# Attention values held still on 32-column tiles: weighing the values with the turned probabilities moving, and turning the heads in 32x32 blocks on VectorE

## The chip, the core and the metric

The kernel runs on one core of a Trainium2 chip. The metric is the device time of one execution in microseconds (us). The kernel before takes 1671.57 us, the median of three runs (1671.38 to 1672.91). A core has TensorE (matrix products, from SBUF into PSUM), VectorE, ScalarE, GpSimd, and SyncE, which issues most transfers. Each works through its own queue in the order in which the program is written, and they meet at semaphores.

## The reference: what is computed

Two layers over `x` (128 sequences of 64 tokens, 128 wide). Each layer adds a gated cross-attention to a context of the same shape and then a gated expert layer. Cut to what matters:

```python
q = (layernorm(x) @ Wq + bq).reshape(b, s, 16, 8)      # 16 heads of 8
k = (ctx @ Wk + bk).reshape(b, s, 16, 8)
v = (ctx @ Wv + bv).reshape(b, s, 16, 8)
attn = softmax(mask(q k^T / sqrt(8)))                  # 64 x 64 for each head
x = x + tanh(g_xattn[l]) * (attn v @ Wo + bo)
# layer 0: each token goes to one of 8 experts, 128 -> 512 -> 128, with gelu
# layer 1: each token has 16 weights w[n,e]; q, k, v = sum_e w[n,e] * (x @ P[e]);
#          one 64 x 64 attention per sequence; out = sum_e w[n,e] * (o @ P_o[e])
x = x + tanh(g_ffn[l]) * experts_l(layernorm(x))
```

Everything is float32 in and out.

## The kernel before

The tokens are worked in 32 units of 256 tokens (4 sequences). The program has three stages. Layer 0's attention is a software pipeline with a loop over the units (`body0` on each engine, which works at once on stages of the units u-2 to u+3). Then come 71 slots of 128 tokens through layer 0's experts. Layer 1 is again a pipeline over units (`body1`), in which the 16 expert projections of a unit (`tokens_parts`, three matmuls of 384 columns for each expert and half unit t) stand on TensorE between the steps of the attention of unit u+2 and of the token attention of unit u-1. The order of everything is written out by hand in these bodies, one for each engine; nothing is scheduled by a planner. The waits are `wait_ge` on a semaphore and a count; `Steps` makes each VectorE step of a chain wait for the one before it.

Of the attention of a unit, these steps bear on the change:

- `head_values` makes the values. The keys' tokens (64 columns of `xcT`) are stationary, and the rows of `m0` are (head parity, key). ScalarE's `copy_v` puts them into `vb`, whose 18 columns for each pair of heads (`VW` = 9 for each head) are 8 dimensions and a column of ones for each of the two heads, and zero in the other head's rows.
- `transpose_probs` turns the exponentials `prob[j]` of one quad of heads (j = 0 to 3) into the bank `tb`, and ScalarE's `copy_pT` copies it to `pT`, of which there are two buffers. So a copy waits until the weighing of two quads before has ended.
- `weigh_values(j)` multiplies: 8 products for each quad, the turned probabilities stationary (128 x 64), 18 columns of `vb` moving, into 64 rows of the bank `po`. Rows of `po` are then (half, query), and its columns are (head, dimension and sum).
- VectorE's `normalise` takes the reciprocal of the sums (`rden`) and multiplies (`on`). TensorE turns `on` (`transpose_heads` in layer 0, `upper_heads` in layer 1), ScalarE copies the result to `oT` (`copy_oT`), and `output` multiplies by `Wo`. VectorE's `add_residual` and `second_stats` take it from there. The statistics go to GpSimd (`second_norm`) and then to ScalarE (`apply_second_norm`).

In `body0` VectorE's last step is `normalise(u)`. Its next body begins with `first_stats` of the unit three further on, whose statistics GpSimd turns into a scale and applies (`norm`, `apply_norm`, into `xn`); TensorE's `transpose_in` waits for that. In `body1`, VectorE's `take_part` adds the t = 0 half of a projection to `qkv` out of one of two banks; `part` on TensorE waits until the part two before it has been taken. `token_weights(u-1)` on VectorE normalises the token attention, and TensorE's `token_weights(u-1)` then turns it.

## Time and profile before

| | |
|---|---|
| time, median of 3 runs | 1671.57 us (1671.38 to 1672.91) |
| profiled execution: span from the first to the last instruction | 1668.5 us |
| around the span, by the median | 3.1 us |
| layer 0's attention: values made (L1639) | 13.8 to 342.5 us |
| layer 1: values made (L1639) | 534.8 to 1536.4 us |
| TensorE busy (matmul) over the span | 1592.5 us (95%) |
| VectorE, ScalarE, GpSimd busy | 1206.6, 1079.6, 1179.4 us |

The profiled execution comes with no time of its own beyond its span. TensorE's share of busy time is no measure of how close it is to its peak, since matmuls overlap in the records; how far apart the starts of two groups lie says what the first one costs in the queue.

### The profile page before, as it was taken

The numbers are of one execution on the slowest core, as the hardware profiler recorded it, in microseconds if no ns is written. First come the engines' busy times: TensorE is split into PE (matmuls) and PEld (weight loads), VectorE is DVE, ScalarE is ACT, GpSimd is POOL, SyncE is SP. The second block draws the span as 40 slices with busy tenths as digits, with TensorE's granted clock in tenths as the row PEclk, the third lists the DMA queues.
The fourth block names the chain that finished last, engine by engine and source line by source line (L and its number), as shares of the span: only waits on it lengthen the run. The fifth ranks groups of instructions, "written<-read, shape, count | busy, mean of one in ns | idle before, by whom it ended". The sixth has DMA issues, their size and how long they took to land.

```text
span 1668.5 us, 50902 instructions
## 1 busy us (share of the span) xinstructions
PE 1592.5 (95%) x15977; PEld 1386.3 (83%) x15978; DVE 1206.6 (72%) x3915; ACT 1079.6 (65%) x2725; POOL 1179.4 (71%) x1715
## 2 busy tenths in 40 slices
PE   6999999976999899999999999999999999999996
PEld 4777777756998689888988988888988988898885
DVE  3677777753554568788887888788888888787785
ACT  3777777743555556666666666666666666666654
POOL 3556656642455578887888888887888888887785
PEclk9999999987999999999999999999999999999998
DMA  2322222234542100000000000000000000000000
GB/s 74 109 73 74 76 75 76 80 96 129 146 134 77 29 17 11 17 17 21 14 18 17 17 18 16 17 16 21 14 18 17 18 17 17 16 16 11 5 8 10
DMA packets 92101, 68.95 MB, mean 41 GB/s; under 512 B 13936, under 2 KB 87696, under 8 KB 91920
## 3 DMA queue, kind: packets, MB, share of 16 engines
q1 hardware_dynamic: 76512, 49.34, 10.1%
q0 software_dynamic: 5120, 12.62, 2.4%
q10 hardware_dynamic: 10288, 4.74, 1.1%
q8 instruction: 94, 1.54, 0.4%
q14 instruction: 87, 0.71, 0.1%
HBM read 35.74 MB, written 22.52 MB: 35 GB/s over the span
## 4 chain that ended last, share of the span: by engine, by line
PE 81%; DVE 5%; issue 5%; POOL 5%; DMA 2%; SPq 1%; ACT 1%; POOLq 0%; DVEq 0%; ACTq 0%
PE s_bank L1884 14%; PE s_bank L1885 12%; PE s_bank L1886 12%; PE po L1702 6%; PE tb L1685 5%; PE po L1831 4%; PE s_bank L1819 4%; PE s_bank L1665 3%; PE s_bank L2034 2%; PE m L1639 1%; PE s_bank L2021 1%; PE tb L1884 1%; POOL sorted_in L652 1%; POOL qkv L726 1%; PE m L1935 1%
## 5 line engine op out<-in xcount | busy, mean ns | idle before, releaser
L726 POOL TENSOR_TENSOR qkv<-qkv,scaled 128x384 f32<-128x384 f32 x480 | 490.1, 1021 | 128.8 <-ACT scaled L1009 91.2
L1009 ACT ACTIVATE scaled<-s_bank,wg 128x384 f32<-128x384 f32 x449 | 257.2, 582 | 128.8 <-PE s_bank L1886 127.3
L1884 PE MATMUL s_bank<-proj_hi,hn_hi 128*128 128x384 f32 x900 | 331.4, 368 | 1.3 <-DVE qkv L1451 1.0
L1451 DVE SCALAR_TENSOR_TENSOR qkv<-s_bank,wg,qkv 128x384 f32<-128x384 f32 x449 | 274.2, 611 | 49.6 <-PE s_bank L1886 37.9
L1885 PE MATMUL s_bank<-proj_lo,hn_hi 128*128 128x384 f32 x900 | 303.7, 337 | 0.0
L1886 PE MATMUL s_bank<-proj_hi,hn_lo 128*128 128x384 f32 x900 | 302.1, 336 | 0.0
L869 ACT ACTIVATE pT<-tb 128x512 f32<-128x512 f32 x256 | 152.2, 595 | 148.9 <-PE tb L1685 81.3
L1884 PEld LDWEIGHTS s_bank<-proj_hi,hn_hi 128*128 128x128 f32 x900 | 169.4, 188 | 16.3 <-ACT scaled L1009 5.9
L1885 PEld LDWEIGHTS s_bank<-proj_lo,hn_hi 128*128 128x128 f32 x900 | 170.0, 189 | 3.0
L1886 PEld LDWEIGHTS s_bank<-proj_hi,hn_lo 128*128 128x128 f32 x900 | 169.0, 188 | 0.0
L1685 PE MATMUL tb<-ident,prob 128*128 128x128 f32 x1024 | 157.6, 277 | 4.8 <-ACT pT L869 4.8
L1702 PEld LDWEIGHTS po<-vb,pT 128*64 128x64 f32 x4096 | 138.8, 138 | 22.2 <-issue 22.2
L1702 PE MATMUL po<-vb,pT 128*64 128x18 f32 x4096 | 151.7, 213 | 0.4 <-ACT pT L869 0.4
L1462 DVE SCALAR_TENSOR_TENSOR halves<-s_bank,wg,halves 128x128 f32<-128x128 f32 x448 | 127.3, 343 | 24.5 <-DVE halves L1462 19.7
L1685 PEld LDWEIGHTS tb<-ident,prob 128*128 128x128 f32 x1024 | 117.8, 141 | 29.3 <-issue 19.9
L726 POOL TENSOR_TENSOR sums<-sums,scaled 128x512 f32<-128x512 f32 x96 | 123.4, 1286 | 12.3 <-ACT scaled L1013 6.0
L1013 ACT ACTIVATE scaled<-s_bank,wg 128x128 f32<-128x128 f32 x384 | 109.5, 368 | 24.1 <-PE s_bank L1886 23.8
L956 ACT ACTIVATE prob<-s_bank 128x512 f32<-128x512 f32 x128 | 73.4, 599 | 76.4 <-PE s_bank L2034 76.4
L927 ACT ACTIVATE hT<-s_bank,b_cols 128x128 f32<-128x128 f32 x284 | 81.2, 367 | 62.6 <-PE s_bank L1819 62.5
L652 POOL DMA_INDIRECT sorted_in<-xr,posi x64 | 66.1, 1033 | 63.8 <-DVE posi L1247 51.0
L1405 DVE TENSOR_REDUCE mx<-s_bank 128x8 fp32r<-128x512 f32 x128 | 79.5, 682 | 40.6 <-PE s_bank L1665 40.6
L1182 DVE RECIPROCAL rden<-po 128x32 f32<-128x32 f32 x64 | 22.8, 357 | 114.7 <-PE po L1702 114.7
(291 smaller groups left out, 3816.2 us busy)
## 6 DMA issues: line engine op xcount, KB each, us to landing
xs<-sorted_in SPq DMA_DIRECT2D x71, 128.5 KB, 2.1
kx<-kT SPq DMA_DIRECT2D x256, 32.0 KB, 1.9
sorted_out<-yo SPq DMA_DIRECT2D x71, 64.0 KB, 1.6
xin<-in_x SPq DMA_DIRECT2D x32, 128.0 KB
cin<-in_ctx SPq DMA_DIRECT2D x32, 128.0 KB
ctx_cols<-xcT SPq DMA_DIRECT2D x32, 128.0 KB
w<-in_L_ffn_W SPq DMA_DIRECT2D x16, 256.0 KB
xcT<-ctx_cols SPq DMA_DIRECT2D x32, 128.0 KB, 2.9
```

The lines of the kernel that those rows point to most:

```text
L652: g.indirect_dma_start(out=sorted_in[:, :], out_offset=bass.IndirectOffsetOnAxis(ap=posi[par][:, t:t + 1], axis=0), in_=xr[par][:, t, 0:RO ...
L726: g.tensor_tensor(into, into, scaled[m % SCALED][:, 0:cols], ALU.add).then_inc(dense_added, 1)
L869: act.activation(pT[j % 2][:, :, :, :], tb[:, :].rearrange("p (r t n) -> p r t n", r=2, t=2), ACT.Copy).then_inc(q["probT_ready"], 1)
L1009: ins = act.activation(into, bank[:, 0:3 * D], ACT.Copy, scale=wg[v % 4][:, 1, k:k + 1])
L1013: ins = act.activation(part[:, cols] if k else sums[:, e, :], bank[:, cols], ACT.Copy, scale=wg[v % 4][:, 1, 4 * k + e:4 * k + e + 1])
L1451: v.scalar_tensor_tensor(out=acc, in0=bank[:, 0:3 * D], scalar=wg[w % 4][:, 0, k:k + 1], in1=acc, op0=ALU.mult, op1=ALU.add).then_inc(dens ...
L1462: ins = v.scalar_tensor_tensor(out=into, in0=bank[:, cols], scalar=wg[w % 4][:, 0, e:e + 1], in1=into, op0=ALU.mult, op1=ALU.add)
L1685: ins = pe.transpose(tb[:, col:col + P], prob[j][:, t, 2 * r:2 * r + 2, :], ident[:, :])
L1702: ins = pe.matmul(po[64 * half:64 * half + 64, col:col + 2 * VW], pT[j % 2][:, t, r, 64 * half:64 * half + 64], vb[par][:, seq, 2 * j + r, ...
L1884: pe.matmul(bank[:, 0:cols], hi[:, tile], of(proj_hi), start=True, stop=False)
L1885: pe.matmul(bank[:, 0:cols], hi[:, tile], of(proj_lo), start=False, stop=False)
L1886: pe.matmul(bank[:, 0:cols], lo[:, tile], of(proj_hi), start=False, stop=True)\
```

## The change

Both layers get the same new weighing. `vb` becomes the stationary operand (18 columns) and the turned probabilities move (64 columns). The output of quad j goes to rows 32j to 32j+17 of `po`, which is a column tile of 32 of the array, and all four quads are weighed in one group of 32 products, after all four copies of `pT` (of which there are now four buffers). `po` then holds the heads already turned, but in blocks: VectorE turns it in 32x32 blocks into `turned` (512 columns, from PSUM), takes the reciprocal, multiplies, and turns the 256 columns of `on` again, straight into `oT`. TensorE's two transposes of `on` and ScalarE's copy of `oT` are gone. `head_values` and `token_scores` make the same products with stationary tiles of 32 columns in place of 64, twice as many. `po` is set to zero once at the start. The PE, ScalarE and VectorE orders are rewritten where the hand-written bodies name these steps; VectorE's `body0` keeps its order.

```diff
-        pT = [sb(f"pT{b}", [P, 2, 2, P]) for b in range(2)]
+        pT = [sb(f"pT{j}", [P, 2, 2, P]) for j in range(QUADS)]
+        turned = sb("turned", [P, 2, 8, 32])
...
             def copy_pT(q, u, j):
                 if exists(u):
                     act.wait_ge(q["probT_in_psum"], 4 * u + j + 1)
-                    wait(act, q["pv_in_psum"], 4 * u + j - 1)
-                    act.activation(pT[j % 2][:, :, :, :], tb[:, :].rearrange("p (r t n) -> p r t n", r=2, t=2),
+                    wait(act, q["pv_in_psum"], u)
+                    act.activation(pT[j][:, :, :, :], tb[:, :].rearrange("p (r t n) -> p r t n", r=2, t=2),
...
             def normalise(q, u):
...
-                    v.wait_ge(q["pv_in_psum"], 4 * u + 4)
-                    step = Steps(v, q["vec_rden"], u, 1)
-                    o = po[:, 0:2 * HEADS * VW].rearrange("p (a c) -> p a c", c=VW)
-                    step(v.reciprocal(rden[:, :], o[:, :, HD]))
-                    wait(v, q["oT_in_psum"], u)
-                    v.tensor_tensor(on[:, :, :].rearrange("p t (h d) -> p (t h) d", d=HD), o[:, :, 0:HD],
-                                    bcast(rden[:, :], HD, 2), ALU.mult).then_inc(q["heads_ready"], 1)
+                    v.wait_ge(q["pv_in_psum"], u + 1)
+                    step = Steps(v, q["vec_heads"], u, 3)
+                    step(v.transpose(turned[:, :, :, :].rearrange("p r b c -> p (r b c)"), po[:, :]))
+                    rows = turned[:, :, :, 0:2 * VW].rearrange("p r b (h c) -> p (r b) h c", h=2)
+                    step(v.reciprocal(rden[:, :, :], rows[:, :, :, HD]))
+                    step(v.tensor_tensor(on[:, :, :, :].rearrange("p r b (h d) -> p (r b) h d", h=2),
+                                         rows[:, :, :, 0:HD], bcast(rden[:, :, :], HD, 3), ALU.mult))
+                    step.end()
+                    wait(v, q["y_in_psum"], u)
+                    v.transpose(oT[:, :, :].rearrange("p t n -> p (t n)"),
+                                on[:, :, :, :].rearrange("p r b c -> p b r c")).then_inc(q["heads_ready"], 1)
...
                     for h in range(2):
-                        ins = pe.matmul(m0[64 * h:64 * h + 64, LEN * seq:LEN * seq + LEN],
-                                        xcT[par][:, 1, LEN * seq:LEN * seq + LEN], by_head[:, h, :, :],
-                                        start=True, stop=True, skip_group_check=True)
+                        for part in range(2):
+                            row, key = 64 * h + 32 * part, LEN * seq + 32 * part
+                            ins = pe.matmul(m0[row:row + 32, LEN * seq:LEN * seq + LEN],
+                                            xcT[par][:, 1, key:key + 32], by_head[:, h, :, :],
+                                            start=True, stop=True, skip_group_check=True)
...
-            def weigh_values(q, u, par, j):
+            def weigh_values(q, u, par):
...
                         for r in range(2):
-                            col = 2 * VW * (8 * t + 2 * j + r)
-                            ins = pe.matmul(po[64 * half:64 * half + 64, col:col + 2 * VW],
-                                            pT[j % 2][:, t, r, 64 * half:64 * half + 64],
-                                            vb[par][:, seq, 2 * j + r, :, :].rearrange("p h c -> p (h c)"),
-                                            start=True, stop=True, skip_group_check=True)
+                            for j in range(QUADS):
+                                col = UNIT * r + LEN * seq
+                                ins = pe.matmul(po[32 * j:32 * j + 2 * VW, col:col + LEN],
+                                                vb[par][:, seq, 2 * j + r, :, :].rearrange("p h c -> p (h c)"),
+                                                pT[j][:, t, r, 64 * half:64 * half + 64],
+                                                start=True, stop=True, skip_group_check=True)
...
-                take(u, "q", 7)
+                token_exp(u - 1)
                 copy_v(q, u + 3, (u + 1) % 2)
-                take(u, "q", 8, 9, 10)
+                take(u, "q", 7, 8, 9, 10)
                 token_weights(u - 1)
-                copy_oT(q, u + 2)
+                take(u, "q", 11, 12)
                 token_heads(u - 1)
...
-                token_max(u - 1)
                 if exists(u + 1):
                     gate_shift(gates)
+                token_max(u - 1)
                 take(u, "q", 8)
+                normalise(q, u + 2)
+                take(u, "q", 9)
                 token_weights(u - 1)
-                take(u, "q", 9)
-                normalise(q, u + 2)
                 total(u - 2)
```

How the instructions stand now is shown by the program's own order (TensorE's queue; an output tile, its operands, the shape; line numbers are those of each kernel's own file). In layer 0's body before, from the turning of the normed input to the second weighing group, `m<-ident,xn` being `transpose_in`, `po<-vb,pT` the weighing and `m<-ident,xr` the turning of the second norm:

```order
L1608 MATMUL m<-ident,xn 128x128 x2
L1610 MATMUL m<-ident,cin 128x128 x2
L1702 MATMUL po<-vb,pT 64x18 x16
...
L1685 MATMUL tb<-ident,prob 128x128 x4
L1674 MATMUL s_bank<-mx,minus_ident 128x512
L1624 MATMUL m<-xcT,wq 128x256
L1625 MATMUL m<-xcT,wk 128x256
L1685 MATMUL tb<-ident,prob 128x128 x4
L1674 MATMUL s_bank<-mx,minus_ident 128x512
L1737 MATMUL m<-ident,xr 128x128 x2
L1674 MATMUL s_bank<-mx,minus_ident 128x512
L1702 MATMUL po<-vb,pT 64x18 x16
```

The same place of the same body in the change:

```order
L1602 MATMUL m<-ident,xn 128x128 x2
L1604 MATMUL m<-ident,cin 128x128 x2
L1681 MATMUL tb<-ident,prob 128x128 x4
L1670 MATMUL s_bank<-mx,minus_ident 128x512
...
L1618 MATMUL m<-xcT,wq 128x256
L1619 MATMUL m<-xcT,wk 128x256
L1681 MATMUL tb<-ident,prob 128x128 x4
L1670 MATMUL s_bank<-mx,minus_ident 128x512
L1721 MATMUL m<-ident,xr 128x128 x2
L1670 MATMUL s_bank<-mx,minus_ident 128x512
L1695 MATMUL po<-pT,vb 18x64 x32
```

The first of the two weighing groups has moved behind the other, and both stand in one group behind the last `tb` of the unit. In layer 1's body before, VectorE's queue from one `take` (L1451) over the token attention's weights (L1428 to L1430) and `normalise` (L1182, L1184) to the take after:

```order
L1451 SCALAR_TENSOR_TENSOR qkv<-s_bank,wg,qkv 128x384
L1428 TENSOR_REDUCE srs<-pbd 128x2
L1429 RECIPROCAL srs<-srs 128x2
L1430 TENSOR_TENSOR pbd<-pbd,srs 128x256
L1451 SCALAR_TENSOR_TENSOR qkv<-s_bank,wg,qkv 128x384
L1182 RECIPROCAL rden<-po 128x32
L1184 TENSOR_TENSOR on<-po,rden 128x256
L1479 TENSOR_TENSOR oall<-halves 128x256
L1451 SCALAR_TENSOR_TENSOR qkv<-s_bank,wg,qkv 128x384
```

And in the change, with the two block transposes (L1171 and L1178):

```order
L1445 SCALAR_TENSOR_TENSOR qkv<-s_bank,wg,qkv 128x384
L1171 STREAM_TRANSPOSE turned<-po 128x512
L1173 RECIPROCAL rden<-turned 128x32
L1174 TENSOR_TENSOR on<-turned,rden 128x256
L1178 STREAM_TRANSPOSE oT<-on 128x256
L1445 SCALAR_TENSOR_TENSOR qkv<-s_bank,wg,qkv 128x384
L1422 TENSOR_REDUCE srs<-pbd 128x2
L1423 RECIPROCAL srs<-srs 128x2
L1424 TENSOR_TENSOR pbd<-pbd,srs 128x256
L1473 TENSOR_TENSOR oall<-halves 128x256
L1445 SCALAR_TENSOR_TENSOR qkv<-s_bank,wg,qkv 128x384
```

Normalising the heads now stands ahead of the token attention's weights and not behind them. On TensorE, the three groups on narrow tiles and the turning of those weights (`m<-ident,pbd`) stand so in layer 1's change, seven projection parts of three rows each lying between the weighing and it (the first of them is shown):

```order
L1635 MATMUL m<-wv,xcT 32x64 x16
L1900 MATMUL m<-qkT 32x64 x8
L1695 MATMUL po<-pT,vb 18x64 x32
L1864 MATMUL s_bank<-proj_hi,hn_hi 128x384
L1865 MATMUL s_bank<-proj_lo,hn_hi 128x384
L1866 MATMUL s_bank<-proj_hi,hn_lo 128x384
...
L1909 MATMUL m<-ident,pbd 128x128 x2
```

Before, `m<-wv,xcT` and the products of `qkT` stood there with the first two weighing groups around the latter, and the other two quads were weighed five parts later.

## Rows read from the trace of the kernel before

**Rows 1.** Busy time by stretch: layer 0, then layer 1 (us; PEclk is the granted clock).
```profile
200.00:300.00 100.00, 97.55 (x1583) 78.64 (x1568) 72.43 (x324) 75.73 (x174) 60.16 (x126) 1.00 0.23 73
1000.00:1100.00 100.00, 100.00 (x871) 88.83 (x870) 81.17 (x234) 68.01 (x173) 82.63 (x105) 1.00 0.06 17
```

**Rows 2.** Timeline of TensorE in one unit of layer 0: start, length of the group.
```profile
201.41 0.44 PE L1608 MATMUL m<-ident,xn 128*128 128x128 f32 x2
...
202.00 1.14 PE L1702 MATMUL po<-vb,pT 128*64 128x18 f32 x32
...
205.93 1.13 PE L1702 MATMUL po<-vb,pT 128*64 128x18 f32 x32
206.88 0.69 PE L1639 MATMUL m<-wv,xcT 128*64 128x64 f32 x16
...
209.78 0.42 PE L1651 MATMUL s_bank<-late_keys,early_rows 32*64 32x512 bf16 x8
210.02 1.04 PE L1665 MATMUL s_bank<-kx,qT 32*64 32x256 f32 x32
210.99 0.66 PE L1685 MATMUL tb<-ident,prob 128*128 128x128 f32 x4
211.60 0.41 PE L1608 MATMUL m<-ident,xn 128*128 128x128 f32 x2
```

**Rows 3.** Timeline of the other engines in the same unit of layer 0.
```profile
203.21 0.88 ACT L861 ACTIVATE xr<-xr,shiftb,rstdb 128x128 f32<-128x128 f32 x2 [0.42 <-POOL shiftb L607]
...
205.46 0.59 ACT L869 ACTIVATE pT<-tb 128x512 f32<-128x512 f32 x1
...
207.10 0.36 DVE L1182 RECIPROCAL rden<-po 128x32 f32<-128x32 f32 x1 [1.68 <-PE po L1702]
...
207.84 0.28 DVE L1145 BATCH_NORM_STATS2 st<-xin 128x6 f32<-128x128 f32 x1
...
208.80 0.19 POOL L604 TENSOR_TENSOR vare<-mv,eps 128x2 f32<-128x2 f32 x1 [0.70 <-DVE mv L1149]
...
210.13 0.48 DVE L1191 SCALAR_TENSOR_TENSOR xr<-m,tg,xb 128x256 f32<-128x256 f32 x1
...
210.57 0.88 POOL L636 TENSOR_SCALAR xn<-xin,rstd,shift 128x128 f32<-128x128 f32 x2 [0.24 <-POOL shift L607]
```

**Rows 4.** Timeline of TensorE in one unit of layer 1.
```profile
1025.04 0.69 PE L1639 MATMUL m<-wv,xcT 128*64 128x64 f32 x16
1025.55 0.65 PE L1702 MATMUL po<-vb,pT 128*64 128x18 f32 x16
...
1026.83 0.44 PE L1884 MATMUL s_bank<-proj_hi,hn_hi 128*128 128x384 f32 x1
...
1031.29 1.13 PE L1702 MATMUL po<-vb,pT 128*64 128x18 f32 x32
1032.35 0.44 PE L1884 MATMUL s_bank<-proj_hi,hn_hi 128*128 128x384 f32 x1
...
1033.50 0.33 PE L1884 MATMUL s_bank<-proj_hi,hn_hi 128*128 128x384 f32 x1
...
1034.02 0.38 PE L1970 MATMUL m<-ident,on 128*128 128x128 f32 x2
1034.24 0.38 PE L1927 MATMUL m<-ident,pbd 128*128 128x128 f32 x2
```

**Rows 5.** Timeline of VectorE in the same unit of layer 1.
```profile
1029.31 0.42 DVE L1428 TENSOR_REDUCE srs<-pbd 128x2 f32<-128x256 f32 x1
...
1030.31 0.61 DVE L1451 SCALAR_TENSOR_TENSOR qkv<-s_bank,wg,qkv 128x384 f32<-128x384 f32 x1
```

**Rows 6.** Groups by line and shape: count, busy us, mean ns of one.
```profile
L1184 DVE TENSOR_TENSOR on<-po,rden 128x256 f32<-128x256 f32 x64 | 27.1, 424 | 2.3
L1411 DVE COPY qkT<-m 128x512 f32<-128x512 f32 x32 | 22.1, 690 | 4.9 <-DVE halves L1462 4.7 <-PE m L1906 0.2
...
L1651 PE MATMUL s_bank<-late_keys,early_rows 32*64 32x512 bf16 x256 | 14.1, 405 | 0.1
```

More of the change, by code:

```diff
@@ L828, in copy_v @@
                     act.wait_ge(q["v_in_psum"], v + 1)
-                    wait(act, q["pv_in_psum"], 4 * v - 4)
+                    wait(act, q["pv_in_psum"], v - 1)
                     for half in range(2):
@@ L867, in copy_pT @@
                     act.wait_ge(q["probT_in_psum"], 4 * u + j + 1)
-                    wait(act, q["pv_in_psum"], 4 * u + j - 1)
-                    act.activation(pT[j % 2][:, :, :, :], tb[:, :].rearrange("p (r t n) -> p r t n", r=2, t=2),
+                    wait(act, q["pv_in_psum"], u)
+                    act.activation(pT[j][:, :, :, :], tb[:, :].rearrange("p (r t n) -> p r t n", r=2, t=2),
                                    ACT.Copy).then_inc(q["probT_ready"], 1)
-            def copy_oT(q, u):
-                if exists(u):
-                    act.wait_ge(q["oT_in_psum"], u + 1)
-                    wait(act, q["y_in_psum"], u)
-                    turned = po if q is s[0] else m0
-                    act.activation(oT[:, :, :], turned[:, 0:256].rearrange("p (t n) -> p t n", t=2), ACT.Copy)\
-                        .then_inc(q["oT_ready"], 1)
             def small_exp(w):
@@ L892, in body0 @@
                 q = s[0]
-                copy_oT(q, u - 1)
                 copy_pT(q, u, 0)
@@ L1074, in _ @@
             apply_norm(1, 2, 0)
-            copy_oT(q, 0)
             exp_bank(1, 0)
@@ L1090, in _ @@
             copy_v(q, 2, 0)
-            copy_oT(q, 1)
             apply_norm(1, 3, 1)
@@ L1917, in token_scores @@
                             seq = slice(LEN * (2 * t + half), LEN * (2 * t + half) + LEN)
-                            ins = pe.matmul(m1[64 * half:64 * half + 64, LEN * t:LEN * t + LEN], qkT[:, 0, seq],
-                                            qkT[:, 1, seq], start=True, stop=True, skip_group_check=True)
+                            for part in range(2):
+                                row, own = 64 * half + 32 * part, seq.start + 32 * part
+                                ins = pe.matmul(m1[row:row + 32, LEN * t:LEN * t + LEN], qkT[:, 0, own:own + 32],
+                                                qkT[:, 1, seq], start=True, stop=True, skip_group_check=True)
                     ins.then_inc(f["s1_in_psum"], 1)
@@ L1962, in upper_values @@
                     head_values(s[1], 1, v % 2)
-            def upper_heads(v):
-                if exists(v):
-                    since((v + 1, s[1]["v_ready"], v + 2), (v - 1, f["gate_logits"], v))
-                    pe.wait_ge(s[1]["heads_ready"], v + 1)
-                    for t in range(2):
-                        ins = pe.transpose(m0[:, P * t:P * t + P], on[:, t, :], ident[:, :])
-                    ins.then_inc(s[1]["oT_in_psum"], 1)
             def upper_in(v):
                 if exists(v):
-                    since((v - 2, s[1]["oT_ready"], v - 1), (v - 1, s[1]["v_ready"], v))
+                    since((v - 1, s[1]["v_ready"], v))
                     pe.wait_ge(s[1]["xn_ready"], v + 1)
```

103 lines of the change are left out of this document (38 added, 65 removed).

## The prediction

> **What bounds the kernel now.** I read the busy time by stretch first. In layer 1 TensorE has no idle time to speak of at the full clock while VectorE stands at 81%; layer 0 has TensorE at 98% and nobody else above 76% [rows 1]. Such shares come from overlapping records, so next I read one unit of each layer in the timeline, by the distances between starts.
>
> Layer 0 goes round in a loop of engines. `transpose_in` starts at 201.41 and again at 211.60, so a unit takes 10.19 us [rows 2]. Call the start of `transpose_in` X and the moment at which VectorE sees the last weighing W. W is 207.10: VectorE had idled 1.68 us for it [rows 3]. From X to W is 5.69 us. From W to the next X is 4.50 us, every step of it waiting for the one before: `normalise` 207.10 to 207.84, `first_stats`, GpSimd at 208.80 (it had waited 0.70 for the statistics), `xn` at 210.57, TensorE at 211.60 [rows 2, 3]. Whatever VectorE does between W and `first_stats` therefore lengthens the unit by its full duration.
>
> In layer 1 the length of a unit is what stands in TensorE's queue. The queue there runs without a gap: parts of 0.52 us (1033.50 to 1034.02), and the narrow groups between them [rows 4].
>
> **VectorE's price, in both layers.** `normalise` takes 0.74 us from start to start now (207.10 to 207.84) [rows 3]. After the change it is a transpose of 512 columns from PSUM, a reciprocal of 32, a product of 256 and a transpose of 256, each waiting for the one before. The trace has no block transpose. Nearest for the first is the copy of 512 columns from PSUM, 0.69; for the second the product of 256, 0.42 [rows 6]. With 0.36 for the reciprocal [rows 3] and 0.42 for the product that is 1.89, say 1.9: it grows by g = 1.16. Bounds: nothing on VectorE over 128 columns and more here is under 0.28 [rows 3], so two transposes add at least 0.56; if a block transpose runs at half the copy's rate, they cost 1.38 and 0.84 and g is 2.3. I take 1.16, since a transpose moves the same elements once.
>
> **TensorE's price for a 32-column tile.** A product in f32 is two instructions, so the groups of 16 and 32 in the rows are 8 and 16 products. The unknown is what 64 moving columns cost with four column tiles. `L1665` sends 256 columns through each of 32 instructions on eight tiles (32x64) in 0.97 us (210.02 to 210.99): 8192 / 8 / 0.97, or 1056 columns in a us for a tile [rows 2]. The values send 64 columns through 16 instructions on two tiles in 0.51 us (1025.04 to 1025.55): 1004 [rows 4]. So a tile takes a column in 1 ns and the tiles run beside each other. Four tiles then need 64 / 4 = 16 ns for an instruction. The other end is that an instruction costs 30 ns whatever the tile, as the weighing does now (205.93 to 206.88 for 32) [rows 2]. I take 16: the eight tiles of `L1651` have records of 405 ns each, and all eight together last 0.42, so their starts lie within 0.02 us [rows 2, 6].
> A rule speaks against it. The Trainium skill, TensorE: Matmul & The Clock Gate, section "Wait — 56ns, not 53.3ns?", has starts of matmuls never closer than about 25 ns, however few columns; its Part 3, on packing, lets tiles follow each other by 4 ns. The eight starts agree with the second. By the first the kernel would end near the rival below.
>
> **Layer 0's sum.** W to X grows by 1.16. The saved `transpose_heads` and `copy_oT` lie elsewhere: `add_residual` starts at 210.13, right behind VectorE's own queue, so `output` is not what it waits for, and it moves back by g as well [rows 3]. X to W: before, the first weighing group (starting 202.00) lay under ScalarE's chain, and the second began at 205.93, while the last `pT` copy, started at 205.46, was still running until 206.05 [rows 2, 3]. That copy stands behind `xr` (203.21), which had waited for GpSimd [rows 3]. So the first group was free, and freeing it saves nothing. Now the whole group waits for the last copy, X + 4.64, and takes 64 x 16 ns = 1.0 and the tail of 0.2 that the group has today (205.93 + 0.95 to 207.10): X + 5.84 in place of 5.69. I take +0.1, since the chain ahead loses a wait or two. A unit grows by 1.26. There are 32 units and 31 steps from one to the next: **+39 us**. More scores lie ahead of `output` now, and VectorE's row maxima wait behind `add_residual`, but they end some 2 us ahead of need.
>
> **Layer 1's sum.** Values, token scores and half of the weighing take 1.79 us now (1025.04 to 1026.83). After the change the values are 32 x 16 ns = 0.51, the scores 16 x 16 = 0.26 and the whole weighing 1.0: 1.77, the same. Gone are the other half, 1.06 (1031.29 to 1032.35), the slower part behind it (1032.35 to 1033.50 is 1.15 for two parts of 0.52, so 0.1) and two transposes, 0.22 (1034.02 to 1034.24) [rows 4]. TensorE's queue is shorter by 1.38.
> But a wait comes with the new order. TensorE's `token_weights` needs the weights from VectorE, whose queue is now: the take of the part behind the weighing, `normalise`, a take, the weights. That is 0.55 + 1.9 + 0.55 + 1.0 (1029.31 to 1030.31) = 4.0 us [rows 5]; a take's record is 0.61 there, and the next starts a little before its end. It begins when that part's last matmul has ended, 0.2 after the next part's start, since records are 0.33 long and lie 0.17 apart [rows 4]. TensorE has six parts for those 4.2 us, 6 x 0.52 = 3.1. It then waits 1.1 us, with seven parts of t = 0 and t = 1, `token_values` and `output` queued behind. Before, the weights were turned long after they were ready. Net: -1.38 + 1.1 = -0.28 for a unit, over 31 steps **-9 us**. ScalarE loses 0.4 us a unit of copying, which nobody waits for.
>
> **The rest.** The prologue of layer 1 weighs two units with nothing beside them: twice g less twice the transposes, copy and handovers, about +1 us. Zeroing `po` lies under the first loads. The experts' stage of layer 0 is untouched. Sum: 39 - 9 + 1 = +31 us. On the profiled execution's span that is 1668.5 + 31 = 1699.5, and the median lies 3.1 above the span: **1703 us**.
>
> **Rivals.**
> - *Starts on narrow tiles no closer than 30 ns.* For it: 30 ns for an instruction in four groups of quite different columns [rows 2, 4]. Against: the eight starts within 0.02. Weighing costs 1.9 in place of 1.0, so layer 0 grows by 2.16 a unit, +67. Layer 1's group is 112 x 30 ns = 3.4 in place of 1.79, so a unit grows by 1.3, +41. Together 1671.6 + 109 = 1781. The skill's 25 ns would make it 1753. Chance 0.2.
> - *Faster: cheap block transposes.* In g the sum is 31 x (g + 0.1) + 31 x (-1.38 + g - 0.06) + 1, which is zero at g = 0.65. Below that the kernel gains. With g = 0.56 it is 1666, with 0.4 1656. For it: the transpose uses one operand and writes each element once. Against: every operation of 256 and more columns here takes 0.4 and more. The same side is reached if layer 1's wait at `token_weights` doesn't come, since TensorE then keeps its 1.38 (-43): 1669. Chance 0.2.
> - *Dear block transposes* (g = 2.3): +74, +27: 1773. Chance 0.08.
> - *No difference*: g between 0.6 and 0.75, or the two layers cancelling in another way. Chance 0.1.
> - My forecast: 0.42, its own range 1688 to 1722.
>
> What can be told from no change is about 0.2%, 3.3 us. Faster 0.2, same 0.1, slower 0.7. The range reaches from the cheap transposes to the dear ones and most of the 30 ns case: 1663 to 1775.
>
> **What would show it.** Layer 0's unit should be 11.4 us, with VectorE 1.9 us from the weighing to `first_stats`, and TensorE idle ahead of `xn` and ahead of the weighing. Layer 1's unit should shrink by 0.3 from its present length, with an idle time of about 1 us ahead of the turning of `pbd`, put down to VectorE. The weighing should be 1.0 us from its start to the next group. The prediction is wrong if the loop of layer 0 isn't ruled by `normalise`, if the block transposes are far from a copy's price, or if the group of 64 instructions takes nearer 2 us than 1.

## The result, and the profile after

The changed kernel takes 1770.92 us (median of 4 runs, 1762.4 to 1775.09) against 1671.63 for the kernel before: a ratio of 1.0587 (95% interval 1.0558 to 1.0616). The forecast was 1703. The direction is right and the range (1663 to 1775) holds, but the loss is 99 us where 31 was forecast. In a later run, beside runs of the kernel before on the same chip, the same kernel took 1768.33 (1.0573, 1.0543 to 1.0604).

The profiled execution spans 1766.5 us, 98.0 more than before. By the starts of `normalise` it divides as follows:

| | before | after | more | forecast |
|---|---|---|---|---|
| layer 0, first to 32nd `normalise` | 324.1 us | 390.2 | 66.1 | 39 |
| between the layers | 194.4 | 195.5 | 1.1 | 0 |
| layer 1, first to 32nd | 1018.7 | 1045.5 | 26.8 | -9 |
| ahead of the first, and behind the last | 131.3 | 135.3 | 4.0 | 1 |

First the busy time by stretch, to be held against [rows 1]. TensorE has become idle in both layers, over a fifth of the time in layer 0 (busy 78.03 us of 100).

```profile
core 0: us, PE busy (x) PEld busy (x) DVE busy (x) ACT busy (x) POOL busy (x), PEclk, DMA share, GB/s
200.00:300.00 100.00, 78.03 (x1425) 58.28 (x1424) 69.09 (x288) 61.00 (x137) 50.06 (x104) 0.97 0.19 63
1000.00:1100.00 100.00, 93.93 (x916) 79.90 (x915) 82.75 (x233) 63.89 (x160) 80.29 (x101) 1.00 0.06 17
```

The page's chain of work that ended last says the same of the whole span, with its shares by engine:

```profile
PE 48%; DVE 24%; issue 14%; POOL 6%; SPq 3%; DMA 3%; ACT 1%; DVEq 1%; POOLq 0%; ACTq 0%
```

VectorE's share was 5% before. Next the prices, from the groups by line and shape (busy us and mean ns of one behind the bar):

```profile
L1695 PE MATMUL po<-pT,vb 128*18 128x64 f32 x4096 | 72.1, 223 | 2.7 <-issue 1.4 <-ACT pT L870 0.5
...
L1171 DVE STREAM_TRANSPOSE turned<-po 128x512 f32<-128x512 f32 x64 | 45.5, 711 | 85.7 <-PE po L1695 76.6 <-issue 9.1
...
L1174 DVE TENSOR_TENSOR on<-turned,rden 128x256 f32<-128x256 f32 x64 | 29.6, 462 | 2.2
L1178 DVE STREAM_TRANSPOSE oT<-on 128x256 f32<-128x256 f32 x64 | 28.5, 445 | 2.2
L1480 DVE SCALAR_TENSOR_TENSOR res<-oall,tg,x 128x256 f32<-128x256 f32 x32 | 28.3, 886 | 0.1
...
L1473 DVE TENSOR_TENSOR oall<-halves 128x256 f32<-128x256 f32 x32 | 17.4, 544 | 0.1
```

The block transposes cost 711 and 445 ns, about what a copy and a product of as many columns cost before (690 and 424 ns [rows 6]). But `res` (L1480), which the change does not touch, has gone from 520 to 886 ns. In the trace of before its group, and that of `oall`, read:

```profile
L1486 DVE SCALAR_TENSOR_TENSOR res<-oall,tg,x 128x256 f32<-128x256 f32 x32 | 16.6, 520 | 0.1
...
L1479 DVE TENSOR_TENSOR oall<-halves 128x256 f32<-128x256 f32 x32 | 14.4, 451 | 0.1
```

**A unit of layer 0**, TensorE's timeline, to be held against [rows 2]:

```profile
242.99 1.12 PE L1661 MATMUL s_bank<-kx,qT 32*64 32x256 f32 x32 [0.61 <-DMA kx<-kT]
...
244.53 0.61 PE L1711 MATMUL m<-wo,oT 128*128 128x128 f32 x4
246.20 0.41 PE L1602 MATMUL m<-ident,xn 128*128 128x128 f32 x2 [1.06 <-POOL xn L637]
...
248.78 1.22 PE L1618 MATMUL m<-xcT,wq 128*128 128x256 f32 x2 [0.77 <-DVE rank L1228]
249.80 1.06 PE L1619 MATMUL m<-xcT,wk 128*128 128x256 f32 x2
...
252.57 1.09 PE L1695 MATMUL po<-pT,vb 128*18 128x64 f32 x64
253.48 0.63 PE L1635 MATMUL m<-wv,xcT 128*32 128x64 f32 x32
```

The weighing lasts 0.91 us to the next group's start (252.57 to 253.48), 14 ns for each of its 64 instructions. There are three waits that [rows 2] do not have: `scores` for the keys' transfer, `transpose_in` for `xn`, `queries_keys` for VectorE's `rank`. From the start of the product with `wq` to the next start it is 1.02 us. In a unit of before it was 0.44:

```profile
214.02 0.59 PE L1624 MATMUL m<-xcT,wq 128*128 128x256 f32 x2
214.46 0.59 PE L1625 MATMUL m<-xcT,wk 128*128 128x256 f32 x2
```

The windows of the changed kernel's trace say why (the figure behind the five engines' busy times is the granted clock):

```profile
245.00:248.50 3.50, 1.78 (x15) 1.21 (x13) 2.92 (x9) 1.11 (x4) 2.15 (x6) 1.00 0.00 0
248.80:252.00 3.20, 3.20 (x10) 2.54 (x11) 1.78 (x8) 2.19 (x6) 1.62 (x2) 0.50 0.36 111
```

TensorE had been busy for half of the first window; in the second the granted clock was 0.50, its lower level, 1.2 GHz in place of 2.4. Between 50 and 400 us the trace shows eight such spells, of 3.4 us each; in the kernel before there was none but the 37.5 us at layer 0's end. The other engines in the same unit, to be held against [rows 3]:

```profile
240.49 0.72 DVE L1171 STREAM_TRANSPOSE turned<-po 128x512 f32<-128x512 f32 x1 [1.97 <-PE po L1695]
...
242.46 0.25 DVE L1135 BATCH_NORM_STATS2 st<-xin 128x6 f32<-128x128 f32 x1
...
245.24 0.48 DVE L1185 SCALAR_TENSOR_TENSOR xr<-m,tg,xb 128x256 f32<-128x256 f32 x1 [0.56 <-PE m L1711]
...
248.42 0.88 ACT L862 ACTIVATE xr<-xr,shiftb,rstdb 128x128 f32<-128x128 f32 x2 [0.96 <-POOL shiftb L608]
...
251.75 0.60 ACT L870 ACTIVATE pT<-tb 128x512 f32<-128x512 f32 x1 [0.23 <-PE tb L1681]
...
253.74 0.72 DVE L1171 STREAM_TRANSPOSE turned<-po 128x512 f32<-128x512 f32 x1 [3.08 <-PE po L1695]
```

`normalise` is 1.97 us long up to `first_stats` (240.49 to 242.46): g is 1.23, where 1.16 was forecast. `add_residual` now comes 4.75 us behind W (240.49 to 245.24) and waits for `output`; before it came 3.03 behind (207.10 to 210.13) and waited for nothing [rows 3]. ScalarE's `xr` waits 0.96 for GpSimd where it waited 0.42.

One unit can mislead, since a low-clock spell sits in this one. So I took the prediction's two stretches, from X (the start of `transpose_in`) to W (the start of `normalise`) and from W to the next X, as means over 24 units (the sixth to the 29th W) from the starts in the timelines. "Spells" are the half-clock spells between 50 and 400 us.

| kernel | X to W | W to X | unit | spells |
|---|---|---|---|---|
| before | 5.75 us | 4.67 | 10.41 | 0 |
| changed | 6.65 | 5.83 | 12.48 | 8 |
| forecast | 5.85 | 5.83 | 11.7 | |

(The forecast's steps, 0.1 and 1.16, are put on the mean unit of before.) W to X is as forecast to the digit. The miss in layer 0 is all in X to W: +0.90 in place of +0.1. The same trace parts it in two. In the 19 of the 24 units without a spell X to W is 6.42 us, in the 5 with one 7.52. So a spell costs 1.1 us where it falls, 0.23 on the mean unit, and the other 0.67 is there in the units whose clock held.

**A unit of layer 1.** TensorE's timeline, to be held against [rows 4]:

```profile
1038.35 0.97 PE L1695 MATMUL po<-pT,vb 128*18 128x64 f32 x56
1040.18 0.31 PE L1695 MATMUL po<-pT,vb 128*18 128x64 f32 x8 [0.85 <-issue]
...
1046.13 0.44 PE L1909 MATMUL m<-ident,pbd 128*128 128x128 f32 x2 [1.79 <-DVE pbd L1424]
```

The 0.85 us that TensorE stands still inside this weighing is rare: 23 weighings of layer 1 have 0.04 on average. The wait at `token_weights` is there, 1.79 us for this matmul. Over 23 units its weight load waits 20.4 us, 0.9 on average, and from the start of the matmul before it to its own it is 0.90 us where it was 0.11; the forecast was a wait of 1.1. But the chain of work, followed through the same unit (start, length, piece), goes on over VectorE from there to the unit's end:

```profile
1041.24 0.62 DVE qkv L1445
1041.86 0.63 DVE turned L1171
...
1044.12 0.57 DVE qkv L1445
...
1045.99 0.95 DVE oall L1473
1046.95 0.53 DVE qkv L1445
...
1054.97 1.10 DVE res L1480
1056.17 0.61 DVE halves L1453 x2
1056.78 0.53 DVE halves L1456 x2
1057.41 0.50 PE s_bank L1864
```

For 16.2 us (1041.24 to 1057.41) VectorE's own queue is the chain; it is idle for no more than 0.2 us at a time, and TensorE takes over only then. So a second wait stands at the parts of the outputs (the weight load of L1864 waits 19.5 us in 23 units until VectorE has taken an output part, L1461).

### The profile page after: what moved, and what is told of

Same layout as the page of the kernel before. It is cut to its first block, busy times and chain, and to the rows that moved or that the text cites. A ratio compares the mean times of both kernels' runs of the same rounds, so it can differ in the third digit from the quotient of the medians.

```text
span 1766.5 us, 53015 instructions
## 1 busy us (share of the span) xinstructions
PE 1560.5 (88%) x17129; PEld 1309.6 (74%) x17130; DVE 1294.1 (73%) x4044; ACT 1071.7 (61%) x2661; POOL 1190.1 (67%) x1715
## 4 chain that ended last, share of the span: by engine, by line
PE 48%; DVE 24%; issue 14%; POOL 6%; SPq 3%; DMA 3%; ACT 1%; DVEq 1%; POOLq 0%; ACTq 0%
PE s_bank L1864 7%; PE s_bank L1866 6%; PE s_bank L1865 6%; DVE qkv L1445 5%; PE tb L1681 4%; PE s_bank L1799 4%; PE po L1811 4%; PE s_bank L1661 3%; DMA kx<-kT 2%; PE po L1695 2%; PE s_bank L2008 2%; SPq L408 1%; DVE res L1480 1%; DVE wg L1387 1%; DVE turned L1171 1%
## 5 line engine op out<-in xcount | busy, mean ns | idle before, releaser
L727 POOL TENSOR_TENSOR qkv<-qkv,scaled 128x384 f32<-128x384 f32 x480 | 495.4, 1032 | 133.8 <-ACT scaled L1001 99.1
L1864 PE MATMUL s_bank<-proj_hi,hn_hi 128*128 128x384 f32 x900 | 330.9, 368 | 14.7 <-ACT scaled L1001 9.6
L1864 PEld LDWEIGHTS s_bank<-proj_hi,hn_hi 128*128 128x128 f32 x900 | 169.3, 188 | 40.0 <-ACT scaled L1001 17.5
L1681 PE MATMUL tb<-ident,prob 128*128 128x128 f32 x1024 | 163.2, 283 | 12.8 <-ACT pT L870 12.7
L1681 PEld LDWEIGHTS tb<-ident,prob 128*128 128x128 f32 x1024 | 123.9, 147 | 44.1 <-issue 35.5
L727 POOL TENSOR_TENSOR sums<-sums,scaled 128x512 f32<-128x512 f32 x96 | 123.4, 1285 | 12.1 <-ACT scaled L1005 5.7
L1864 PE MATMUL s_bank<-proj_hi,oh_hi 128*128 128x512 f32 x256 | 106.8, 417 | 15.0 <-DVEq L1461 12.8
L1171 DVE STREAM_TRANSPOSE turned<-po 128x512 f32<-128x512 f32 x64 | 45.5, 711 | 85.7 <-PE po L1695 76.6
L653 POOL DMA_INDIRECT sorted_in<-xr,posi x64 | 66.1, 1033 | 61.3 <-DVE posi L1241 47.9
L1866 PE MATMUL s_bank<-proj_hi,oh_lo 128*128 128x512 f32 x256 | 101.4, 396 | 0.0
```

The source lines that it names most:

```text
L727: g.tensor_tensor(into, into, scaled[m % SCALED][:, 0:cols], ALU.add).then_inc(dense_added, 1)
L1681: ins = pe.transpose(tb[:, col:col + P], prob[j][:, t, 2 * r:2 * r + 2, :], ident[:, :])
L1864: pe.matmul(bank[:, 0:cols], hi[:, tile], of(proj_hi), start=True, stop=False)
L1866: pe.matmul(bank[:, 0:cols], lo[:, tile], of(proj_hi), start=False, stop=True)\
```

## The experiments

Each was run in a batch together with the kernel before; a time in brackets is that kernel's in the same batch. These times of the kernel before differ by some 3 us, but for the first batch.

**The first batch** had four edits of the changed kernel. All came out far above it, and the kernel before itself took 1773.45 us in it in place of 1672. So its times say nothing of the edits, and the four were run again. What was written ahead of it:

`stats_first`:


> Layer 0 alone: VectorE takes the statistics of the next unit ahead of normalise instead of behind it. Theory A (normalise lies in the loop from the weighing to the next transpose_in): 2.0 us of normalise leave the loop, other waits take up part, so 1.2 to 1.9 us a unit, 31 steps, 37 to 59 us below 1770.9: 1712 to 1734. Theory B (the new order on TensorE and the clock, not normalise, lengthened layer 0): at most 10 us, 1760 or more.

`double_l0`:


> Layer 0 alone: the first block transpose of normalise (0.71 us in the trace, some 0.06 us of handover) is done twice. Theory A (normalise in the loop, each us of it a us of the unit): 31 x 0.77 = +24 us, 1795. Theory B (another chain sets the unit): less than 10 us more.

`rank_early`:


> Layer 0 alone, order of TensorE: output ahead of scores and router_rank ahead of the third transpose_probs, as they stood in the kernel before. Theory C (part of the growth that was not forecast comes from queries_keys waiting for VectorE's router_rank, and scores for the keys' transfer behind it): 0.5 to 0.9 us a unit, 15 to 27 us less, 1744 to 1756. Theory A alone (only normalise and the weighing): no change, within 5 us.

`l1_weights_first`:


> Layer 1 alone: VectorE does token_weights ahead of the take of part 9 and normalise behind it, the order of the kernel before; TensorE's order stays the new one. Theory D (the 1.8 us that TensorE waits at token_weights is what normalise ahead of it costs): TensorE gets 1.5 us of it back, 31 units, up to 45 us less, 1726. Theory E (VectorE's own work now sets layer 1's unit, so the wait only moves to another product): within 10 us of 1770.9. In between if output waits for the later heads.

Measured, in this order: 1820.98, 1848.73, 1817.10 and 1805.56 (1773.45). The last edits layer 1 alone, but its layer 0 took 13.6 us a unit in place of 12.5. TensorE's timeline of one of its weighings:

```profile
254.73 0.79 PE L1695 MATMUL po<-pT,vb 128*18 128x64 f32 x41
...
255.73 0.30 PE L1695 MATMUL po<-pT,vb 128*18 128x64 f32 x3 [0.21 <-issue]
...
256.70 0.31 PE L1695 MATMUL po<-pT,vb 128*18 128x64 f32 x4 [0.66 <-issue]
...
257.43 0.42 PE L1695 MATMUL po<-pT,vb 128*18 128x64 f32 x14 [0.42 <-issue]
```

Inside the group TensorE stands still three times and waits for nothing that the trace shows. In layer 0 of this run its idle time inside the weighings adds up to 36 us, and the starts lie some 55 us further apart in sum; in the changed kernel's own trace no such idle time is there.

**The changed kernel again, and the kernel before again.**

> The changed kernel itself, nothing edited, beside the four edits that each came out 32 to 75 us above it. Theory F (the stalls of 0.2 to 0.9 us inside layer 0's weighing, 54 us in the run that edits layer 1 alone, are not made by the edits; they come and go with something the source does not show): this run shows them too in its profile or its times lie up to 50 us above 1771. Theory G (the edits cause them): no such stalls, 1771.

> The kernel before the change, unedited, on this chip: 1671.6 within 0.2%, with the weighing of each unit free of stalls inside.

Measured: 1768.33 and 1671.29 (1673.56), with no stall in the weighings of layer 0. So the stalls belong to that batch and not to the change. In every later batch the kernel before took 1670 to 1674. What made the stalls is open.

**Statistics ahead of `normalise`**, in the changed kernel and in the one before (with the line at the body's start gone, and the first unit's ahead of the loop):

```diff
                 max_quad(q, u + 1, 3)
+                first_stats(0, u + 3, 1 - par)
                 normalise(q, u)
```

> The kernel of stats_first once more, since in that call the kernel before the change itself took 1773 us in place of 1672, so that its times can't stand beside 1771. Theory A (normalise lies in the loop from the weighing to the next transpose_in): 1712 to 1734. Theory B (order and clock lengthened layer 0): 1760 or more. The same edit to the kernel before gave nothing (1675 against 1674), so the gain may also stop at what that kernel's other chains allow, a unit of 11 us or more.

> The kernel before the change, with the statistics of the next unit ahead of normalise in layer 0. If the loop from the weighing over normalise and first_stats to transpose_in sets its unit, normalise's 0.74 us leaves it and the unit falls by 0.3 to 0.7 us: 1650 to 1662. If not, 1671.6 within 5 us, or slower.

Measured: 1770.11 (1670.48) and 1675.13 (1673.56): nothing gained in either. In the changed kernel W to X falls from 5.83 to 4.05, as it should when 1.9 us leave it, but X to W grows from 6.65 to 8.55. The waits of the stretch 200 to 300 us show where it went (us in total, times, longest):

```profile
POOL vareb L605 <- DVE mvb L1139: 26.5, 8, 3.5
ACT xr L862 <- POOL shiftb L608: 17.0, 8, 2.2
```

GpSimd's second norm now waits 3.3 us a unit for `add_residual` and `second_stats`, and ScalarE waits for GpSimd. So `normalise` lies in a second loop as well: `normalise`, `output`, `add_residual`, `second_stats`, GpSimd, ScalarE's `xr`, and behind it in ScalarE's queue the last two `pT` copies, the weighing, `normalise`. Taking it out of the one loop leaves it in the other. The clock has a part in it too: 20 half-clock spells lie between 50 and 400 us in place of 8. But in the 8 of 24 units without one X to W is still 7.97 us, and in the kernel before, which has no spell there, the same edit takes W to X from 4.67 to 4.24 and X to W from 5.75 to 6.41. So the second loop holds without the clock.

**One transpose twice**, in layer 0:

```diff
+                    if extra:
+                        step(v.transpose(turned[:, :, :, :].rearrange("p r b c -> p (r b c)"), po[:, :]))
```

> The kernel of double_l0 once more, for the same reason. Theory A (each us of normalise is a us of the unit): 31 x 0.77 = +24 us, 1793. Theory B: less than 10 us more.

Measured: 1800.50 (1670.48), 30 to 32 us over the changed kernel for 31 x 0.77 = 24 us of work. Theory A holds: W to X grows by just the 0.77 us of work, from 5.83 to 6.60. The slope is above one, since X to W grows as well, by 0.39. All of the 24 units have a half-clock spell in that stretch, where 5 had one in the changed kernel. This is the likely cause; no run shows it by itself.

**Where `output` and `router_rank` stand on TensorE:**

```diff
+                output(0, u - 1)
                 scores(0, u + 1, 1 - par)
                 transpose_probs(q, u, 1)
-                output(0, u - 1)
...
+                router_rank(u - 2)
                 transpose_probs(q, u, 2)
                 subtract_max(q, u + 1, 0)
-                router_rank(u - 2)
```

> The kernel of rank_early once more, for the same reason. Theory C (queries_keys waiting for router_rank and scores for the keys' transfer cost 0.5 to 0.9 us a unit): 1742 to 1754. Theory A alone: 1769 within 5 us.

Measured: 1757.23 (1670.48), 11 to 14 us less. X to W is 5.91, within 0.1 of the forecast's 5.85. But W to X rose to 6.31, and ten half-clock spells had moved there: 1.36 us of each unit's W to X was at 1.2 GHz. It is 6.96 us in the 10 units with a spell and 5.84 in the 14 without, the changed kernel's 5.83.

**The same, with TensorE kept busy** ahead of `output`:

```diff
+                    for _ in range(6):
+                        pe.matmul(s_bank[0][:, :], onesb[:, :], bcast(onesb[:, :], 4, 1), start=True, stop=True)
                 output(0, u - 1)
```

> The kernel of rank_early, with six bf16 products of 512 columns (0.21 us each at the full clock, written to a bank that is free there, not used) in TensorE's queue ahead of output, where it waits 1.6 us a unit. In rank_early 1.4 us a unit from normalise to transpose_in ran at half clock. Theory K (idle time there lowers the clock, and that costs 0.7 us a unit): fewer half-clock spells and 10 to 20 us less than rank_early's 1757. If the clock costs nothing on the path: the same or, where six products are too many, up to 10 us more.

Measured: 1744.89 (1673.32), 12 us less than without the six products. Layer 0's windows, first of `rank_early_2`, then of this kernel:

```profile
200.00:300.00 100.00, 81.84 (x1458) 59.60 (x1443) 71.83 (x299) 61.84 (x141) 52.62 (x110) 0.96 0.19 63
```

```profile
200.00:300.00 100.00, 90.95 (x1592) 63.78 (x1591) 72.62 (x300) 65.26 (x147) 52.14 (x106) 1.00 0.22 71
```

Not one half-clock spell is left between 50 and 400 us. X to W is 5.99, W to X 5.83, the unit 11.83. That is the forecast's unit of 11.7 but for 0.1.

**g alone, in the kernel before:**

```diff
+                        step(v.transpose(scrap[:, :], po[:, :]))
+                        step(v.transpose(scrap[:, 0:256], po[:, 0:256]))
                     step(v.reciprocal(rden[:, :], o[:, :, HD]))
```

> The kernel before the change, with two block transposes (512 and 256 columns, 0.71 + 0.45 us by the trace, each waiting for the one before) put into layer 0's normalise ahead of the reciprocal; their result is not used. That is the prediction's g = 1.16 us alone, without the new order, tiles and weighing. If g alone lengthens layer 0, the stretch from normalise to the next transpose_in grows by 1.2 us and the rest by 0.1: 31 x 1.2 to 1.3, 1709 to 1713. If the late output, residual and second norm lengthen the other stretch too whatever the order (0.9 us, as in the changed kernel): 1735 to 1740.

Measured: 1713.72 (1673.32), +40.4 us. X to W is 5.69, unchanged, so with the old order the longer `normalise` leaves that stretch alone. W to X is 6.21, 1.54 more and not 1.16: this run too has eight half-clock spells in layer 0's pipeline, where the kernel before has none. In the 17 of 24 units whose W to X has no spell it is 5.80 (+1.13), in the 7 with one 7.19. So g costs its own length, some 35 us over 31 steps, and the rest of the 40 is the clock. That the sum meets the forecast's 39 is in part luck.

**SyncE's order**: the next unit's load behind the placing of the keys, alone and with the other edits of layer 0.

```diff
+                if exists(u + 2):
+                    store_context(u + 2, par)
+                    place_keys(0, u + 2)
                 if exists(u + 3) and not (isinstance(u, int) and u < -1):
...
                     load_unit(u + 3, 1 - par)
-                if exists(u + 2):
-                    store_context(u + 2, par)
-                    place_keys(0, u + 2)
```

> Layer 0 alone, SyncE's order: the context's store and the placing of the keys ahead of the load of the next unit. Theory H (layer 0's longer unit is a loop through SyncE: scores, output, residual, GpSimd's second norm and xb, the load that waits for xb, the keys' transfers queued behind it, scores): 0.5 to 1.5 us a unit, 15 to 45 us below 1769: 1724 to 1754. If only normalise on the way to transpose_in counts: 1769 within 5 us.

> Layer 0 alone, all order edits together: output ahead of scores, router_rank earlier, statistics ahead of normalise, keys placed ahead of the load. Each loop that the traces show is opened once. Theory H: unit 10.7 to 11.3 us in place of 12.6, so 1710 to 1728. If the new operations' own time sets the unit (VectorE and TensorE), it stays over 12: 1750 or more.

Measured: 1812.45 and 1879.75 (1673.18). Both edits fail, and badly: the load itself is now late. In the stretch 200 to 300 us VectorE waits 4.2 us for it in `sp_keys_first`. In `l0_orders` it waits 37, and TensorE behind VectorE:

```profile
DVE st L1135 <- DMA xin<-in_x: 37.0, 6, 6.3
PEld m L1714 <- DVE lg L1196: 29.0, 6, 5.1
```

I had put one chain right by lengthening another. Theory H is neither shown nor refuted by it: an order in which neither the load nor the keys are late was not tried.

**Narrow tiles alone**, in the kernel before:

```diff
-                        ins = pe.matmul(m0[64 * h:64 * h + 64, LEN * seq:LEN * seq + LEN],
-                                        xcT[par][:, 1, LEN * seq:LEN * seq + LEN], by_head[:, h, :, :],
...
+                        for part in range(2):
+                            row, key = 64 * h + 32 * part, LEN * seq + 32 * part
+                            ins = pe.matmul(m0[row:row + 32, LEN * seq:LEN * seq + LEN],
+                                            xcT[par][:, 1, key:key + 32], by_head[:, h, :, :],
...
```

> The kernel before the change, with head_values and token_scores alone on tiles of 32 columns (32 and 16 instructions in place of 16 and 8, 14 ns each in place of 30). By the 14 ns of the changed kernel's trace the groups last as long as before (0.45 and 0.23 us): within 5 us of 1671.6. If starts on narrow tiles cost 30 ns, layer 0 and layer 1 grow by 0.5 to 0.7 us a unit: 1700 or more.

Measured: 1681.73 (1673.56), ratio 1.0051 (1.0034 to 1.0068). Small, but not nothing. In TensorE's timeline of a unit of layer 1, beside [rows 4]:

```profile
1029.98 0.65 PE L1641 MATMUL m<-wv,xcT 128*32 128x64 f32 x32
1030.57 0.67 PE L1704 MATMUL po<-vb,pT 128*64 128x18 f32 x16
1031.16 0.43 PE L1922 MATMUL m<-qkT 128*32 128x64 f32 x16
1031.52 0.67 PE L1704 MATMUL po<-vb,pT 128*64 128x18 f32 x16
```

From start to next start, as means over 23 units, the four groups read:

| | before | `narrow_only` | changed kernel |
|---|---|---|---|
| values (narrow) | 0.51 us | 0.58 | 0.47 |
| first weighing group (tiles of 64) | 0.44 | 0.60 | |
| token scores (narrow) | 0.26 | 0.36 | 0.23 |
| second weighing group (tiles of 64) | 0.58 | 0.60 | |

In `narrow_only` the four grow by 0.35 us together. Layer 1's queue is full, and its median unit goes from 34.02 to 34.38. But the narrow groups are not what is dear: the weighing groups, whose instructions were left alone, grow as well, and in the changed kernel, where the values, the scores and the weighing all stand on 32-column tiles and follow one another, the same two narrow groups take less than before. So the price seems to go with a group on 32-column tiles standing beside one on tiles of 64, and the changed kernel doesn't pay it in layer 1.

**Layer 1, two orders of VectorE.** First in the changed kernel:

```diff
                 take(u, "q", 8)
-                normalise(q, u + 2)
-                take(u, "q", 9)
                 token_weights(u - 1)
+                take(u, "q", 9)
+                normalise(q, u + 2)
```

> The kernel of l1_weights_first once more, for the same reason. Theory D (TensorE's wait at token_weights is what normalise ahead of it costs): up to 45 us less, 1725. Theory E (VectorE's own work sets layer 1's unit, the wait moves): within 10 us of 1769. Layer 0 must be that of the changed kernel, 12.6 us a unit; if it is not, this call is disturbed too.

Measured: 1760.90 (1670.48), 7 to 10 us less. The wait at `token_weights` is gone (no such row is left), but the weight loads of the parts wait 21.9 us for VectorE's takes where they waited 12.2. Theory E.

Then the change in layer 1 alone (layer 0 with the old functions and order), and that with the order above and with `total` and `result` of two units ago ahead of the weighing:

> The change in layer 1 alone; layer 0 has the functions, tiles and order of the kernel before. By the traces layer 1 and its ends hold 27 + 5 + 1 us of the 98: 1700 to 1706 against 1671. If layer 1 suffers only from what layer 0 leaves behind (the clock at its entry, late loads), under 1685.

> The layer 1 change alone, with two more moves on VectorE: token_weights ahead of take 9 and normalise behind it, and total and result of two units ago ahead of the weighing (VectorE idles 1.6 us a unit for parts there). Theory E (from the weighing's end to the last take VectorE's queue, 16.5 us without a gap, sets layer 1's unit): the two operations of 0.4 to 1.0 us leave that stretch, 1.2 to 2 us a unit less than the layer 1 change alone, so 1640 to 1668. If TensorE's queue sets the unit, nothing more than the 8 us that token_weights first gave: 1692 or more.

Measured: 1700.84 and 1685.75 (1673.18). Layer 1's change costs 27.7 us by itself (21.8 of it between layer 1's first and 32nd `normalise`, where the changed kernel has 26.8 more), so most of it is not what layer 0 leaves behind. The moved work gives back 15, less than the 33 or more that theory E said. The waits of `hybrid_tuned` from 700 to 1500 us show what comes next:

```profile
PEld s_bank L1924 <- ACT scaled L1012: 25.7, 21, 1.8
PE s_bank L1924 <- ACT scaled L1012: 19.1, 21, 1.5
PEld s_bank L1924 <- DVE qkv L1468: 18.5, 71, 0.6
```

With VectorE shorter there, TensorE waits 25.7 us for the other half's accumulation, ScalarE and GpSimd, where it waited 15.2 in `hybrid`. The median unit is 34.11 in place of 34.62, still over the 34.02 of before. No version that I ran beats the kernel before.

## Why the prediction was right and wrong

- **g, right.** Forecast 1.16, measured 1.23 in one unit and 1.22 as the mean of 24; a block transpose costs about what a copy of as many columns costs. `pad_before` shows the consequence by itself: W to X grows by 1.13 where the clock does not fall. Its +40 us, beside a forecast of 39, hold the clock as well, so that match proves less than it seems.
- **The narrow tile, right.** 16 ns for an instruction was forecast and 14 measured, 0.91 us for the group of 64. The rival at 30 ns is refuted. By the Trainium skill, TensorE: Matmul & The Clock Gate, section "Wait — 56ns, not 53.3ns?", it would have been 25; the trace disagrees with that for four tiles side by side. The sum of "the same" for layer 1's three groups holds too: forecast 1.77, and 0.47 + 0.23 + 1.01 = 1.71 us in the changed kernel (the last is the median; the rare stall is left out). The 8 us of `narrow_only` come where narrow and wide tiles meet, and are no part of the miss.
- **Layer 0, X to W, wrong.** The step that failed: "More scores lie ahead of `output` now, and VectorE's row maxima wait behind `add_residual`, but they end some 2 us ahead of need." I looked at the maxima and not at what else hangs on `add_residual`. The second norm does, over GpSimd, and ScalarE's `xr` for it stands ahead of the last two `pT` copies. The prediction even cites this `xr` waiting for GpSimd. `add_residual` comes 4.8 us behind W on average where it came 3.2 behind, so it moved back by 1.6, not by g. With `output` ahead of `scores` again it comes 4.4 behind and X to W is 5.91 (`rank_early_2`), and with the old order and g alone 5.69 (`pad_before`). `rank_early_2` moves `router_rank` too; which of the two moves gave how much was not tried.
- **The clock, missing altogether.** I costed waits as waits. More idle time on TensorE brought 3.4 us spells at 1.2 GHz, in which its work on the path takes twice as long: a stretch with a spell in it is 1.1 us longer than one without (X to W in the changed kernel, W to X in `rank_early_2`). Filling one wait gave 12 us back (`rank_early_busy`).
- **Layer 0's sum of parts.** From the first to the 32nd `normalise` the profiled executions take 324.1 us (before), 364.3 (`rank_early_busy`), 374.2 (`rank_early_2`) and 390.2 (changed). So 40 remain with the order put right and no spell in the way, the forecast's 39; taking the six products out again adds 10, and the new order 16: the 66. The last two steps are not pure, since the order also decides where the spells fall.
- **Layer 1, wrong in sign.** The wait at `token_weights` came at its size (0.9 for 1.1). The step that failed is what stood on it: "TensorE's queue is shorter by 1.38", less that one wait. VectorE's next 16.2 us have hardly a gap, so there the unit is not TensorE's queue any more. VectorE's growth behind the weighing counts there, and the 1.38 us are idle time. Taking the wait away gave 7 to 10 us, not 28, and shortening VectorE's stretch as well gave 15. That is less than a chain of VectorE alone would give, so what sets the rest of layer 1's unit is open; by its waits, ScalarE and GpSimd come next.
- **Layer 1's VectorE grew by more than g.** `res` went from 520 to 886 ns, `oall` from 451 to 544, the product of `pbd` from 426 to 513: 0.55 us a unit that was not costed. For `res` the cause is the GpSimd instruction beside it, see below. How much of the 27 us this growth makes was not tried.
- **Prologue and tail**: forecast +1, measured some +5, in part perhaps the four half-clock spells at layer 1's entry, which the kernel before does not have.

The rival that ended on the other side, cheap transposes, is refuted by their price.

## What to carry to other kernels

When a step moves back, list everything that waits for it, on every engine, and follow each to the queue in which it stands ahead of something needed; opening one loop helps only if the step isn't in a second. Where TensorE just fills the unit, an engine at 80% is the next bound, and if its work behind one barrier has no gap then a saving on TensorE can be worth nothing, as here. And a wait on TensorE costs more than its length once the clock falls. This holds in an experiment that is meant to isolate another cost as well, so sort the units by whether the clock fell in them before you read a mean.

## What the runs showed of the hardware

- A block transpose of f32 on VectorE: 711 ns for 128 x 512 from PSUM, 445 ns for 128 x 256 within SBUF.
- Four column tiles of 32 side by side: four starts within some 20 ns, then the next four 56 ns after the first, 14 ns for an instruction. Where such a group stood beside one on tiles of 64, both got longer: by 0.35 us for four groups of `narrow_only`, whose narrow groups take 0.58 and 0.36 us, against 0.47 and 0.23 in the changed kernel among their like.
- VectorE's operations on two SBUF operands stretch, but only beside GpSimd. In the changed kernel's layer 1 the two `res` with no GpSimd work beside them took 485 ns; in 29 others GpSimd was in the middle of an addition (L727) when `res` started, with 0.65 us of it left on average, and `res` took 927. Each of the 29 ended 281 to 289 ns after that addition did. In the kernel before, 25 of the 32 `res` started with only 0.14 to 0.17 us of such an addition left, and took 473 to 478; in the 4 that met more of it they again ended 279 to 283 ns behind it. So the whole stretch is the rest of the GpSimd instruction that is already running, and the change made it longer by shifting VectorE's queue against GpSimd's. The Trainium skill, SBUF — State Buffer, section "SBUF: two separate sides", has such an operation and a GpSimd operation that reads SBUF lock each other out for a whole instruction; the trace agrees.
- A kernel can run 6% longer in all executions of a batch: the kernel before took 1773 us in one and 1674 in the next, on the same chip. Its granted clock was 0.97 in place of 0.98. By that some 106 us ran at the lower level in place of some 60, which makes 23 us at most (an estimate from the two clocks), not 100. The stalls inside groups of small matmuls, shown above, were seen in the edited kernels of that batch; of the kernel before no trace was kept there, so whether it had them is not known. That it was run beside the others is what gave the batch away.
